# Own tiles picked out of the batch tiles by selector weights, in place of a normalisation and transposition of their own

## What is computed

```
xn = _layernorm(x, axis=-1)
latent = xn @ Wc_down                                # 1024 -> 512
q = (latent @ Wq_up).reshape(B, T, 16, 64)
k, v = split(latent @ Wkv_up)                        # 64 and 64, shared by the heads
y = softmax(causal(q k^T / 8)) v ;  s = y @ Wc_proj
h = silu(xn @ wg^T) * (xn @ wu^T)                    # hidden 3072, weights int / 127
g = _silu(h @ wd^T)
return x + s * g
```

## Time and profile before

| | us |
|---|---|
| two timed runs | 3459.2 and 3423.29, median 3441.24 |
| the profiled execution | 3424.08 |
| its span on the slowest core (core 1) | 3422.5 |
| spans of the eight cores | 3388.2 to 3422.5 |
| busy: TensorE matmul, VectorE, ScalarE, GpSimd | 2208.4, 1185.2, 1330.9, 412.8 |

### The profile page before, as it was taken

The page is one execution under the profiler, slowest core; times in us unless marked ns, Lnnn a source line. Parts: engine busy times, 40 slices in busy tenths (PEclk is TensorE's granted clock), DMA queues, the critical chain, the costliest instruction groups (busy, mean ns, idle before and its releaser), DMA issues.

```text
span 3422.5 us, 34012 instructions; the slowest of 8 cores (3388.2 to 3422.5 us)
## 1 busy us (share of the span) xinstructions
PE 2208.4 (65%) x10592; PEld 1045.3 (31%) x10592; DVE 1185.2 (35%) x2154; ACT 1330.9 (39%) x1489; POOL 412.8 (12%) x329
## 2 busy tenths in 40 slices
PE   1333545456576585685758758587575888588986
PEld 1211323221341352352225322252222442223421
DVE  3555443432532434425243241432423321411211
ACT  0112222221331342342634436344465437375365
POOL 0111212123143000100000000000000000000000
PEclk9556767676886797897879968799797887788877
DMA  5031246649395252362015300153000350011510
GB/s 97 33 70 45 40 78 79 107 69 157 50 111 74 64 131 79 84 152 78 33 39 115 115 14 33 39 131 99 14 33 13 84 140 32 21 26 44 144 30 13
DMA packets 549452, 240.57 MB, mean 70 GB/s; under 512 B 476576, under 2 KB 532896, under 8 KB 549280
## 3 DMA queue, kind: packets, MB, share of 16 engines
q1 hardware_dynamic: 431952, 195.27, 21.9%
q0 software_dynamic: 117328, 43.14, 11.9%
HBM read 250.00 MB, written 27.26 MB: 81 GB/s over the span
## 4 chain that ended last, share of the span: by engine, by line
PE 40%; DVE 20%; DMA 14%; issue 11%; ACT 10%; POOL 4%; DVEq 1%; SPq 0%; ACTq 0%; POOLq 0%
PE ps_y L548 10%; PE ps_sc L561 9%; ACT p_sb L572 7%; PE ps_u L719 5%; PE ps_u L726 5%; PE ps_u L790 3%; DVE recbf L600 3%; POOL p_sb L580 3%; DMA wd_t<-wdbf 3%; DMA wu_t<-wu 2%; DVE stat L299 2%; DMA wd_t<-wd 2%; PE ps_u L638 2%; ACT xn_t L308 2%; DVE xnT L371 2%
## 5 line engine op out<-in xcount | busy, mean ns | idle before, releaser
L572 ACT ACTIVATE p_sb<-ps_sc 128x1024 bf16<-128x1024 f32 x1088 | 1094.9, 1023 | 1423.5 <-PE ps_sc L561 1410.8
L548 PE MATMUL ps_y<-p_sb,vaug_sb 128*65 128x512 bf16 x2176 | 753.0, 432 | 221.8 <-POOL p_sb L580 132.1
L561 PE MATMUL ps_sc<-qs,kT_sb 65*128 65x512 bf16 x2176 | 752.2, 432 | 25.0 <-DVE qs L529 25.0
L580 POOL TENSOR_TENSOR p_sb<-p_sb,masks_sb 128x1024 bf16<-128x1024 bf16 x128 | 272.9, 2140 | 2390.0 <-ACT p_sb L572 2389.8
L548 PEld LDWEIGHTS ps_y<-p_sb,vaug_sb 128*65 128x65 bf16 x2176 | 214.7, 121 | 663.3 <-issue 590.8
L790 PE MATMUL ps_u<-wd_t,h_sb 128*128 128x512 bf16 x768 | 237.3, 441 | 143.5 <-DMA wd_t<-wd 59.4
L561 PEld LDWEIGHTS ps_sc<-qs,kT_sb 65*128 65x128 bf16 x2176 | 222.1, 107 | 243.0 <-issue 124.0
L719 PE MATMUL ps_u<-xnT_own,wg_t 128*128 128x256 bf16 x1536 | 230.8, 301 | 77.7 <-DVE h_sb L737 58.8
L364 PE MATMUL ps_u<-ident_sb,xn_t 128*128 128x128 bf16 x640 | 75.7, 256 | 255.6 <-DVE xn_t L329 217.6
L590 DVE CAST yf<-ps_y 64x1024 bf16<-64x1024 f32 x32 | 38.8, 1213 | 571.8 <-PE ps_y L548 571.8
L726 PE MATMUL ps_u<-xnT_own,wu_t 128*128 128x256 bf16 x1536 | 224.5, 295 | 9.6 <-DMA wu_t<-wu 9.4
(11 more groups left out here) (88 smaller groups left out, 1394.0 us busy)
## 6 DMA issues: line engine op xcount, KB each, us to landing
wg_t<-wgbf SPq DMA_DIRECT2D x144, 256.0 KB, 3.7
wu_t<-wubf SPq DMA_DIRECT2D x144, 256.0 KB, 4.0
wd_t<-wdbf SPq DMA_DIRECT2D x288, 128.0 KB, 2.2
xt<-xb SPq DMA_DIRECT2D x64, 512.0 KB, 4.8
xo_t<-xo SPq DMA_DIRECT2D x32, 512.0 KB, 4.2
wg_t<-wg POOLq DMA_DIRECT2D x48, 256.0 KB, 7.3
wu_t<-wu POOLq DMA_DIRECT2D x48, 256.0 KB, 7.8
wd_t<-wd POOLq DMA_DIRECT2D x96, 128.0 KB, 3.9
```

What stands on the lines that cost most here:

```text
L548: last = O("tensor", lambda e_, t=t, nh=nh, par=par: e_.matmul(ps_y[0:65, nh * 512:(nh + 1) * 512], vaug_sb[:, t, :], p_sb[:, par, nh * 51 ...
L561: sct = O("tensor", lambda e_, t=t, nh=nh, sb2=sb2: e_.matmul(ps_sc[:, sb2 * 1024 + nh * 512:sb2 * 1024 + (nh + 1) * 512], kT_sb[0:65, t * ...
L572: ex = O("scalar", lambda e_, sb2=sb2: e_.activation(p_sb[:, sb2, :], ps_sc[:, sb2 * 1024:(sb2 + 1) * 1024], AF.Exp), [sct, st["p_war"][sb ...
L580: mtoks[t] = O("gpsimd", lambda e_, pview=pview, mj=mj: e_.tensor_tensor(pview, pview, masks_sb[:, mj, :].unsqueeze(1).broadcast_to([128, ...
```

## The change

The own tile is no longer loaded, normalised and transposed for the attention and FFN. It is one of the group's four batch tiles, and which one is known per core: a new input `sel` (128x4) has a 1 in the column of that tile and 0 in the others (the program is the same on all cores). After the transposition of batch tile q of a group, VectorE reads `ps_u` a second time: for q = 0 it writes `sel[0]` times it to the own tile's part of `xnT_own`, for q = 1, 2, 3 it adds `sel[q]` times it there (`scalar_tensor_tensor`, in place). `ps_u` is released only after that. The queries can be made only after the fourth tile, so `gen_latq_q` moves behind the K/V block of pair 2, directly ahead of `emit_latq_m`. The own tile's item on `vecq` goes; a third item, `tail`, only queues these two. The combination still loads `xo`.

```diff
+        O("sync", lambda e: e.dma_start(sel_sb[:, :], sel_d[:, :]), out="wF", dma=True)
...
             ev = O("vector", lambda e: e.tensor_copy(
                 dst_ap, ps_u[:, :].rearrange("p (k n) -> p k n", k=DK)),
                 [mts[-1]], out="v")
             st["util"] = ev
+            if acc is not None:
+                q, g = acc
+                dstv = xnT_own[:, :, g * 128:(g + 1) * 128]
+                srcv = ps_u[:, :].rearrange("p (k n) -> p k n", k=DK)
+                if q == 0:
+                    a2 = O("vector", lambda e, dstv=dstv, srcv=srcv, q=q:
+                           e.tensor_scalar_mul(dstv, srcv, sel_sb[:, q:q + 1]),
+                           [mts[-1], st["xnown_war"], t_misc], out="v")
+                else:
+                    a2 = O("vector", lambda e, dstv=dstv, srcv=srcv, q=q:
+                           e.scalar_tensor_tensor(dstv, srcv, sel_sb[:, q:q + 1],
+                                                  dstv, ALU.mult, ALU.add),
+                           [mts[-1], st["xnown_war"], t_misc], out="v")
+                st["xnown_war"] = a2
+                st["util"] = a2
+                if q == 3:
+                    xown_done[g] = a2
...
-        def emit_own_tile(e):
...
         def enqueue_group(g):
-            def own_item(g=g):
-                emit_own_tile(g)
-                tq_must.append(lambda: gen_latq_q(g))
...
+            def tail(g=g):
+                tq_must.append(lambda: gen_latq_q(g))
                 tq_must.append(lambda: (emit_latq_m(g), None)[1])
-            vecq.append(own_item)
             vecq.append(pair1)
             vecq.append(pair2)
+            vecq.append(tail)
...
+        "sel": np.tile(np.eye(4, dtype=np.float32)[3 - i], (128, 1)),
```

More of the change, by code:

```diff
@@ L135, in build_program @@
     masks_d = nc.dram_tensor("masks", [4, 128, 128], BF16, kind="ExternalInput")
+    sel_d = nc.dram_tensor("sel", [128, 4], F32, kind="ExternalInput")
     out_d = nc.dram_tensor("out", [OWN, D], F32, kind="ExternalOutput")
@@ L326, in ln_flush @@
             st["ln"] = b
-            for x_ap, xn_out_ap, dst_ap, gi, waits, done_aff, done_tp, a in ln_pend:
+            for x_ap, xn_out_ap, dst_ap, gi, waits, done_aff, done_tp, a, acc in ln_pend:
                 aff = O("vector", lambda e, x_ap=x_ap, xn_out_ap=xn_out_ap, gi=gi:
@@ L335, in ln_flush, with submit_ln @@
                 tq_must.append(lambda aff=aff, xn_out_ap=xn_out_ap, dst_ap=dst_ap,
-                               done_tp=done_tp: gen_transposes(xn_out_ap, dst_ap,
-                                                               [aff], done_tp))
+                               done_tp=done_tp, acc=acc: gen_transposes(
+                                   xn_out_ap, dst_ap, [aff], done_tp, acc))
             ln_pend.clear()
-        def submit_ln(x_ap, xn_out_ap, dst_ap, waits, done_aff, done_tp, flush=False):
+        def submit_ln(x_ap, xn_out_ap, dst_ap, waits, done_aff, done_tp,
+                      flush=False, acc=None):
             gi = len(ln_pend)
             a = emit_ln_stats_a(x_ap, waits, gi)
-            ln_pend.append((x_ap, xn_out_ap, dst_ap, gi, waits, done_aff, done_tp, a))
+            ln_pend.append((x_ap, xn_out_ap, dst_ap, gi, waits, done_aff,
+                            done_tp, a, acc))
             if flush or len(ln_pend) == 2:
```

21 lines of the change are left out of this document (5 added, 16 removed).

## The result

The kernel after ran in 3442.17 us (median of 17 runs, 3430.99 to 3481.16), the kernel before, on the same chip beside it, in 3422.16 (median of 16, 3409.7 to 3468.41). The ratio is 1.007, with a 95% interval of 1.0049 to 1.009: the change makes the kernel 0.7% slower, about 24 us. More runs of the same kernel put it at 3422: of the 16, only that 3459 and a 3468 lie above 3433.

What follows compares the result with a forecast made beforehand. No engine is full; what counts is where TensorE stands still, and VectorE's queue sets a group's head. Groups 3 to 15 +17, start -5, groups 1 and 2 +3: +15 on 3424.08 gives 3439 us, range 3385 to 3495.

Steps and rivals of the forecast that it cites:

- The head: Start of a group's preparation, first reduction to ps_u release: 36.3 us falls to 23.5, saving 12.8 a group.
- The queries, moved: Queries behind tile 3's K/V: 8.1 us a group taken, the full-clock lower bound; 11.7 at low clock the upper.
- 1.5 of cold aftermath: Behind the queries' block of gaps, two attention steps at low clock: 1.5 us more a group.
- The selections: VectorE's second read of ps_u: 1.22 us each, all showing on TensorE; three beyond the head, 3.7 a group.
- The rival in which they are free: TensorE held by something else at each hand-over, so selections and clock terms cost nothing: 3344 us, chance 0.07.
- The clock: Stretch behind the head: longer waits lower TensorE's granted clock; 1.5 us a group taken, half of 3.1.
- the upper bound: Clock term's upper end: 20 us of matmul work at 0.82 instead of 0.94 costs 3.1 us a group.
- A group: Groups 3 to 15, all terms of one group's preparation summed: +1.3 us each, times 13, +17.
- The start: From the first reduction to the first attention matmul: 71.1 us becomes 65.6, saved 5.
- Groups 1 and 2: Two short early slots at low clock: +2.9 us each, half taken because mask multiplications cover some, +3 together.
- Queues and engines: VectorE, ScalarE and SP loads: queries' small transfers behind FFN weight loads costed at nothing; 3 us a group without cover.
- The verdict: Whole kernel: 3439 us is no change against the median 3441; within 2%, 68 us, given 0.80.

Runs made afterwards that it cites:

- a_selx: Kernel after, but selections read the copy in xnT (SBUF) and ps_u is released behind the copy: 3348.51 us, 0.9812 of before.
- a_esx: Kernel after with first FFN step forced at tick 12 and selections reading xnT, ps_u released behind the copy: 0.9722 of before.
- a_early: Kernel after with one FFN step, which issues the first weight loads, forced at tick 12 as before the change: 3422.94 us, 1.0019 of before.
- c_all2: Kernel after, early FFN loads, selections from xnT; from slot 5 seven attention steps before the first pair, eight after each pair: 3211.61 us, 0.9402 of before.
- a_skip2: Kernel after with early FFN loads, selections on PSUM; from slot 5 seven attention steps before first pair, eight after each: 0.9698 of before.
- a_dbl: Kernel after with a second read of ps_u into a scratch tile behind each selection, before the release: 3594.62 us, 1.0516 of before.

## Why the prediction was right or wrong

**The head: right.** 23.9 measured, 23.5 predicted, against 36.3 before. TensorE's wait for the normalised tile is 15.2 a group (15.4 predicted), that for tile 0's selection 11.4 (11). The wait for latT did not vanish: 26.0 in 16 groups, 1.6 each, where I wrote near 1.

**The queries, moved: right in size.** 8.2 in slot 11, where I took 8.1 and bounds of 8.1 to 11.7. Over all 16 groups the two runs of 32 matmuls take 4.7 where slot 11 has 3.9 and the low clock 7.1, so some groups pay a part of the difference. The 1.5 of cold aftermath is seen there too, in the FFN step behind them (1.91 and 1.22 for eight matmuls each, where a warm one takes 1.04).

**The selections: right.** 64 of them at 1276 ns; hand-overs of 1.25 to 1.47 where I said about 1.5. The rival in which they are free was priced at 3344, 95 us under the forecast; taking them off `ps_u` brought 88 (a_selx against after) and 101 (a_esx against a_early, and again c_all2 against a_skip2). As a statement about the change that rival was wrong, since TensorE does wait. As a price it was good, with some luck: it left out tile 0's selection, and it dropped the 1.5 behind the queries, which a_selx still shows.

**The clock: right over the kernel, absent in the slot that I looked at.** The window around the stretch behind the head has 0.82, the number that I used for the upper bound, but that window takes in part of the wait; the stretch alone has 0.91, and a_selx, without the waits, 0.85. So in slot 11 the waits of the change do not lower it, and the 3.2 us that three selections cost are no more than their own time. Slot 11 is one of the cheapest, though: on the median core a_selx is 5.2 us shorter there and 7.3 to 9.0 in slots 3 to 7. The mean over slots 2 to 13 is 6.7, of which four selections of 1.28 are 5.1. The 1.6 that is left agrees with what TensorE's busy time says. The matmuls are the same, but they take 2146.3 us in the kernel after and 2120.3 in a_selx (medians of the eight cores), 26 us or 1.6 a group less, because more of them run at the full clock. Between c_all2 and a_skip2 it is 37.5 us. a_dbl shows that the term grows fast once the holds are twice as long.

**A group: right in size, but not shown to be so by its terms.** +1.3 predicted, +1.0 measured, the mean of twelve slots. In a_early the same twelve slots are 0.3 each below before (2591.1 against 2594.6), so up to the whole of the +1.0 can be the moved FFN step, which the sum for a group did not hold. **The start: right.** From the first reduction of group 0 to that of group 1 it is 66.9 us instead of 71.9, the 5 that were predicted; another 1.6 lie ahead of the first reduction.

**Groups 1 and 2, and "Queues and engines": this step failed.** I put +3 on the two short slots together and cost the queues at nothing, on the ground that "three weight slots are loaded ahead". In slot 1 that cover does not exist: it is the slot in which these three are loaded for the first time, by GpSimd, between its mask multiplications. The change moved that first FFN step by four ticks, behind four more masks, and SP's in-order queue passed the delay on to `yT`. Slot 1 lost 14.6. I had looked at what each queue carries in a steady group and never laid the first slots' order on GpSimd and SP side by side, although the order of instructions shows the move without any run. a_early settles it: with the step back at its tick, slots 0 and 1 together are 3.0 us longer than before, the +3 that I had put on them. So the term that failed is the nothing for the queues, which is 12.4 us in one slot and perhaps more in later ones.

**The verdict: wrong for a second reason, and by itself enough.** The sum was made against the profiled execution (3424) and came out at +15. I then compared it to the median of two runs, 3441, and read "no change". The middle of two runs that lie 36 us apart is no centre; 14 more runs put it at 3422. Nor is 2% what a measurement of this kernel can tell from no change: the interval came out at 0.2% to either side. Held to the profiled execution, or to the lower of the two runs, the same sum says slightly slower, as it was. The outcome to which I had given 0.80, within 2%, is the one that came, since 0.7% lies within.

## What to carry to other kernels

A read added ahead of a buffer's release cost about its full length here, and more where the hold let TensorE's clock fall; let it read the copy instead of the original, even if it isn't faster there. When a step is moved or dropped, compare the order on every engine in the first occurrence as well as in a steady one, down to the queues of GpSimd and SP: what is prefetched in every later slot has to be loaded for a first time once. And when a gap is to be filled with other work, look at what the work that fills it itself needs from the engine that is late: a long instruction such as the 6.54 us reciprocal of this kernel reaches TensorE through a second in-order engine.

## What the runs showed of the hardware that I had not expected

The cost of a hold is not linear: three selections of 1.28 us cost 3.2, three more 6.4, as the granted clock of the stretch went 0.85, 0.91, 0.69 (in mean over the span, on the slowest core, 0.805, 0.790 and 0.758).

A `scalar_tensor_tensor` of 1024 elements takes the same time from bf16 in SBUF as from float32 in PSUM (1294 against 1276 ns), while a `tensor_scalar` goes from 1276 to 486. These are the rows of a_selx:

```profile
L390 DVE SCALAR_TENSOR_TENSOR xnT_own<-xnT,sel_sb,xnT_own 128x1024 bf16<-128x1024 bf16 x48 | 62.1, 1294 | 6.0 <-DVE xnT L376 0.9
...
L386 DVE TENSOR_SCALAR xnT_own<-xnT,sel_sb 128x1024 bf16<-128x1024 bf16 x16 | 7.8, 486 | 1.8 <-DVE xnT L376 0.2
```

The Trainium skill (VectorE: DVE Perf Modes, "The perf-mode tier table") caps a `tensor_scalar` that reads PSUM at a slower mode than one on bf16 in SBUF, and the second row agrees. It gives a two-input `tensor_tensor` a faster mode on bf16 in SBUF; the first row, another two-input operation, shows no such gain.
